# Loads of a graph kernel asked for in small parts, two small jobs moved off GpSimd

## The reference, cut to what matters

```python
N_NODES = 3125; N_EDGES = 103125; EMB = 128; EDGE_F = 16     # dst sorted; every node has its own edge too
def _gin_conv(x, src, dst, edge_attr, w1, b1, bn_w, bn_b, w2, b2, ew, eb):
    edge_emb = edge_attr @ ew.T + eb
    agg_x = segment_sum(x[src], dst, n) + x
    agg_e = segment_sum(edge_emb, dst, n) + eb
    h = concatenate([agg_x, agg_e], axis=1) @ w1.T + b1
    h = (h - mean) * rsqrt(var + BN_EPS) * bn_w + bn_b       # over the nodes
    return relu(h) @ w2.T + b2
h = maximum(layernorm(x), 0)
for l in range(5): h = _gin_conv(h, ...); if l < 4: h = relu(h)
return x + h
```

## Time and profile before

| | |
|---|---|
| median of 3 runs | 663.9 us (662.63 to 664.17) |
| profiled execution, its own time | 669.72 us |
| its span | 667.9 us |
| PE busy, share of the span | 90% |
| DVE, ACT, POOL busy | 50%, 39%, 11% |
| granted TensorE clock, mean | 0.968 |

### The profile page before, as it was taken

The page is one execution under the profiler, slowest core; times in us unless marked ns, Lnnn a source line. Parts: engine busy times, 40 slices in busy tenths (PEclk is TensorE's granted clock), DMA queues, the critical chain, the costliest instruction groups (busy, mean ns, idle before and its releaser), DMA issues.

```text
span 667.9 us, 12631 instructions
## 1 busy us (share of the span) xinstructions
PE 602.1 (90%) x5319; PEld 370.4 (55%) x5319; DVE 331.5 (50%) x663; ACT 260.9 (39%) x569; POOL 71.9 (11%) x90
## 2 busy tenths in 40 slices
PE   4788798969999887999997999997999998999976
PEld 3666687745555544844446644456544458444456
DVE  6897999989999817422113421124411225101034
ACT  0277967746676716502115411127211227012142
POOL 5450136500222100000000000000000000000000
PEclk9798999998999988999998999998999998999999
DMA  6980000000000000100000100000100000100033
GB/s 189 315 227 6 2 4 27 6 5 3 5 4 3 4 6 1 28 5 1 1 2 1 32 1 1 2 1 1 32 1 1 1 2 1 32 1 1 1 98 96
DMA packets 13320, 19.22 MB, mean 29 GB/s; under 512 B 2263, under 2 KB 7397, under 8 KB 13251
## 3 DMA queue, kind: packets, MB, share of 16 engines
q1 hardware_dynamic: 12099, 16.00, 7.9%
q0 software_dynamic: 1152, 2.20, 1.5%
HBM read 16.26 MB, written 1.60 MB: 27 GB/s over the span
## 4 chain that ended last, share of the span: by engine, by line
PE 59%; DVE 2%; ACT 1%; issue 0%; POOLq 0%; DVEq 0%
PE bank L1309 39%; PE bank L1373 10%; PE bank L1345 8%; PE bank L1339 2%; ACT h L1426 1%; DVE bn_stats L1530 1%; DVE h L1551 0%; DVE h L1552 0%; PE bank L1356 0%; PE bank L251 0%; DVE h L1571 0%; ACT bn_small L1439 0%; DVE bn_small L1545 0%; DVE bn_small L1544 0%; DVE bn_small L1546 0%
## 5 line engine op out<-in xcount | busy, mean ns | idle before, releaser
L1309 PE MATMUL bank<-adj,h_pieces 128*128 128x504 bf16 (+1 forms) x1372 | 263.5, 351 | 0.0
L1309 PEld LDWEIGHTS bank<-adj,h_pieces 128*128 128x128 f16 x1372 | 123.0, 97 | 141.4 <-issue 10.2
L1530 DVE BATCH_NORM_STATS2 bn_stats<-bank 128x6 f32<-128x504 f32 (+1 forms) x70 | 42.8, 627 | 220.3 <-PE bank L1345 219.7
L965 ACT ACTIVATE adj<-bank 128x450 bf16<-128x450 f32 x175 | 95.4, 548 | 67.5 <-PE bank L828 54.3
L1417 ACT ACTIVATE aggT<-bank 128x504 f32<-128x504 f32 x24 | 14.2, 590 | 261.0 <-PE bank L1345 223.7
L852 PE MATMUL bank<-h,adj 128*17 128x40 f32 (+11 forms) x1752 | 78.8, 205 | 16.8 <-DVE h L638 11.7
L443 DVE TENSOR_TENSOR h<-iota_lo,h 128x1536 bf16<-128x1536 bf16 (+2 forms) x95 | 87.5, 921 | 8.3 <-PE bank L828 7.2
L828 PE MATMUL bank<-h 128*128 128x75 bf16 x1064 | 69.2, 201 | 19.7 <-DVE h L443 17.3
L452 PE MATMUL bank<-adj,h_pieces 128*128 128x450 bf16 x343 | 83.4, 355 | 1.6 <-issue 1.6
L828 PEld LDWEIGHTS bank<-h 128*128 128x128 bf16 x1064 | 55.0, 99 | 51.0 <-DVE h L443 30.4
L1373 PE MATMUL bank<-weights,h 128*128 128x128 f32 (+1 forms) x500 | 66.7, 302 | 18.3 <-DVE h L1552 18.3
(11 more groups left out here) (145 smaller groups left out, 332.0 us busy)
## 6 DMA issues: line engine op xcount, KB each, us to landing
adj<-attr SPq DMA_DIRECT2D x1, 2524.5 KB
adj<-attr SPq DMA_DIRECT2D x1, 1963.5 KB, 15.3
weights<-wpack SPq DMA_DIRECT2D x5, 323.0 KB
out<-h SPq DMA_DIRECT2D x6, 256.0 KB
adj<-attr SPq DMA_DIRECT2D x1, 1402.5 KB, 7.4
adj<-attr SPq DMA_DIRECT2D x2, 561.0 KB, 5.1
h<-mpack SPq DMA_DIRECT2D x5, 179.0 KB
adj<-order SPq DMA_DIRECT2D x2, 202.0 KB, 3.3
```

Of the source, the lines that this page charges most:

```text
L965: nc.scalar.activation(out_view(u), bank_view(n % CNT_BANKS), ACT.Copy).then_inc(s_ev, 1)
L1309: last = nc.tensor.matmul(agg_ps[b][:, 0:w], hp[:, k, s, :], adj[:, k, c * LW:c * LW + w], start=(k == 0 and s == 0), stop=stop and s == p ...
L1530: V.bn_stats(stats[:, h, ds(c * 6, 6)], w1_ps[b][h][:, 0:cols]).then_inc(st_last if last and h == 1 else st_done, 1)
```

## The change

1. Attributes: 13 parts of two tiles. Parts 0 and 1 as before, part 2 where the old part 2 was; each later part, of tiles from k, is asked for by SyncE when TensorE has done attribute step 3k-12.
2. x: the host lays it out by partition and pads it, so that a load is contiguous in each partition. Four parts (6, 6, 6 and 7 tiles), asked for after steps 6, 8, 10 and 12; ScalarE waits part by part. The memset of the last tile goes. At the end x_res is one transfer.
3. The stores of the starts and the loads of the ranges are issued after step 24, the picked columns after step 38; the weights after all that.
4. GpSimd asks for `rows(b)` when strip 2(b-2) is counted, for `pairs(b)` when strip 2(b-2)+5 is. `block_starts(b)` moves from strip b+6 to 2(b-2)+5, `keys(b)` from 2b+14 to 2(b-2)+12, for b from 2 to 8.
5. Own edges: `add_own` and its waits go. TensorE adds them in PSUM: one or two matmuls at the end of each strip's counts (197 in all, 77 of them in strips 0 to 68), the identity as weights, 18 columns of a padded identity as moving operand.
6. `low_piece` 0 to 5 goes to VectorE, at strips 42, 46, ... 62.
7. `edge_weights_f` of the later layers shares memory with `bound_parts`.

```diff
-ATTR_PARTS = ((0, 2), (2, 4), (4, 9), (9, 16), (16, 25))
+ATTR_PARTS = [(k, min(k + 2, NODE_TILES)) for k in range(0, NODE_TILES, 2)]
+X_PARTS = ((0, 6), (6, 12), (12, 18), (18, 25))
+ATTR_AHEAD, X_EVERY, STARTS_AFTER = 12, 2, 24
+def rows_strip(b):
+    return 2 * (b - 2)
 def starts_strip(b):
-    return b + 6 if b >= 2 else -1
+    return rows_strip(b) + 5 if b >= 2 else -1
+def pairs_strip(b):
+    return rows_strip(b) + 5
 def keys_strip(b):
-    return 2 * b + 14 if b >= 2 else 3
+    return rows_strip(b) + 12 if b >= 2 else 3
...
                     sp.wait_ge(s_pair[0], 16)
-                    attr_rows(2)
-                    sp.wait_ge(s_zero, 1)
-                    sp.dma_start(x_st[:, 0:NODE_TILES - 1, :], ...
-                    sp.dma_start(x_st[0:LAST_ROWS, NODE_TILES - 1, :], ...
-                    for m in range(3, len(ATTR_PARTS)):
-                        attr_rows(m)
+                    parts = 2
+                    for i in range(STEPS):
+                        if parts < len(ATTR_PARTS) and i == max(3 * ATTR_PARTS[parts][0] - ATTR_AHEAD, 0):
+                            if i > 0:
+                                sp.wait_ge(s_step, i)
+                            attr_rows(parts)
+                            parts += 1
+                        for j in range(len(X_PARTS)):
+                            if i == LEAD + X_EVERY * j:
+                                sp.wait_ge(s_step, i)
+                                x_rows(j)
+                        if i == STARTS_AFTER:
+                            store_starts()
+                        if i == PICK_AT + LEAD:
+                            spread_picks()
...
-                    for b in range(2, BLOCKS):
-                        rows(b)
-                    for b in range(2, BLOCKS):
-                        pairs(b)
-                    n = 0
                     for u in range(STRIPS):
+                        for b in range(2, BLOCKS):
+                            if u == rows_strip(b):
+                                pool.wait_ge(s_cnt, strip_at(u) + 1)
+                                rows(b)
+                            if u == pairs_strip(b):
+                                pool.wait_ge(s_cnt, strip_at(u) + 1)
+                                pairs(b)
...
-                        if u >= NORM_AT + 4 and (u - NORM_AT) % 4 == 0 and (u - NORM_AT) // 4 < UNITS:
-                            low_piece((u - NORM_AT) // 4 - 1)
-                        while n < len(PIECES_OWN) - 1 and PIECES_OWN[n][2] <= (u + 1) * SC:
-                            add_own(n)
-                            n += 1
... VectorE
+                        i = (u - NORM_AT - 6) // 4
+                        if (u - NORM_AT - 6) % 4 == 0 and 0 <= i < UNITS - 1:
+                            dve.wait_ge(s_hi, i + 1)
+                            V.tensor_tensor(units(hp, i)[:, :, 1, :], units(x_st, i), units(hp, i)[:, :, 0, :],
+                                            ALU.subtract).then_inc(hp_done, 1)
... TensorE, at the end of counts(), own = u
+                        if own is not None:
+                            to = cnt_ps[n % CNT_BANKS][:, 0:SG * AW].rearrange("p (g k m) -> p g k m", g=SG, m=GW)
+                            for k in range(own * SC // P, min((own * SC + SC - 1) // P, NODE_TILES - 1) + 1):
+                                at = SC + own * SC - k * P
+                                last = nc.tensor.matmul(to[:, :, k, :], ident, ident_pad[:, at:at + SC], start=False, stop=True,
+                                                        skip_group_check=True)
                         last.then_inc(s_cnt, 1)
```

More of the change, by code:

```diff
@@ L178, in ln_tiles @@
     return range(2 * (u - at), min(2 * (u - at) + 2, NODE_TILES)) if at <= u else ()
[L181 to L190, removed]
 def agg0_steps(u):
@@ L222, in gin_program @@
         mp = h1[:, 0, COLS - MP_COLS:COLS]
-        ident = sb(whole, "ident", [P, P], BF16)
+        ident_pad = sb(whole, "ident", [P, 2 * SC + P], BF16)
+        ident = ident_pad[:, SC:SC + P]
         m6 = sb(whole, "edge_weights", [SK, HID], BF16)
@@ L400, in gin_program @@
             s_attr = [sem(f"attr_rows{m}_loaded") for m in range(len(ATTR_PARTS))]
-            s_x = sem("x_loaded")
-            s_zero = sem("x_pad_zeroed")
+            s_x = [sem(f"x{j}_loaded") for j in range(len(X_PARTS))]
             s_diag_m = sem("piece_matrices_made")
@@ new lines, in store_starts @@
+                    def store_starts():
+                        sp.wait_ge(s_start, BLOCKS)
+                        sp.dma_start(starts[0:BLOCK0].rearrange("(p b) -> p b", b=1), start_i[0:BLOCK0, 0:1]).then_inc(s_sdram, 16)
+                        for b in range(1, BLOCKS):
+                            sp.dma_start(starts[base_of(b):base_of(b) + GB].rearrange("(p b) -> p b", b=1),
+                                         start_i[0:GB, b:b + 1]).then_inc(s_sdram, 16)
+                        sp.wait_ge(s_sdram, 16 * BLOCKS)
+                        sp.wait_ge(s_step, 3 * SPARE_ROWS)
+                        for at, out in ((0, first_e), (1, next_e)):
+                            sp.dma_start(out, starts[at:at + GROUPS].rearrange("(c j) -> c j", c=CHUNKS)).then_inc(s_ranges, 16)
@@ L495, in _ @@
+                    assert parts == len(ATTR_PARTS)
                     sp.dma_start(wp[:, :], wpack[0]).then_inc(l_wp, 16)
                     sp.dma_start(mp, mpack[0]).then_inc(l_mp, 16)
[L499 to L511, removed]
@@ L534, in _ @@
                                    allow_small_or_imprecise_dtypes=True).then_inc(s_thr, 1)
-                    nc.gpsimd.memset(x_st[:, NODE_TILES - 1, :], 0.0).then_inc(s_zero, 1)
-                    nc.gpsimd.memset(ident[:, :], 0.0).then_inc(s_ident0, 1)
+                    nc.gpsimd.memset(ident_pad[:, :], 0.0).then_inc(s_ident0, 1)
                     nc.gpsimd.memset(ones[:, :], 1.0)
@@ L818, in transposes, with counts @@
                         last.then_inc(s_tr, 1)
-                    def counts(n, batch, first, tiles):
+                    def counts(n, batch, first, tiles, own=None):
                         pe.wait_ge(s_oh, batch + 1)
@@ L872, in _ @@
                             transposes(BLOCKS)
-                        counts(strip_at(u), batch_at(u), u % PAIR * SG, SG)
+                        counts(strip_at(u), batch_at(u), u % PAIR * SG, SG, u)
                         if u + LEAD < STEPS:
@@ L989, in _ @@
                         for k in ln_tiles(u, SUMS_AT):
-                            if k == 0:
-                                act.wait_ge(s_x, 32)
+                            for j, (a, _) in enumerate(X_PARTS):
+                                if k == a:
+                                    act.wait_ge(s_x[j], 16)
                             nc.scalar.activation(x_st[:, k, :], x_st[:, k, :], ACT.Copy, accum_out=ln_sum[:, k:k + 1]
@@ L1626 @@
     first = np.ascontiguousarray(dst_lin[WIN::WIN].reshape(1, FIRSTS))
+    nodes = np.zeros((NODE_TILES * P, D), np.float32)
+    nodes[:N_NODES] = np.asarray(x)
+    nodes = np.ascontiguousarray(nodes.reshape(NODE_TILES, P, D).transpose(1, 0, 2)).reshape(P, NODE_TILES * D)
     w1, w2 = np.asarray(L0_gnn_W1), np.asarray(L0_gnn_W2)
@@ L1653 @@
     arrays = {
-        "x": np.ascontiguousarray(x), "first": first, "dst_lin": dst_lin, "pair": pair, "order": order,
+        "x": nodes, "first": first, "dst_lin": dst_lin, "pair": pair, "order": order,
         "dst_win": dst_win,
```

45 lines of the change are left out of this document (13 added, 32 removed).

## The result

The changed kernel took 669.8 us in the median of five runs (666.7 to 671.6), the kernel before 662.9 in as many beside it; the ratio of the two is 1.0076, with an interval from 1.0058 to 1.0094. So the change makes the kernel slower, by 5.0 us as the ratio has it (the two medians lie 6.9 us apart; what follows goes by the ratios). The prediction was 660.8 us, faster.

A forecast was written before the change was run, and what follows sets the result against it. VectorE was taken to bound the first stage from 18 to 138 us, TensorE from 158 to 232. Terms -4.7 +0.7 -2.2 +0.8 +3.3 -0.4 -0.6 gave -3.1, so 663.9 became 660.8 us, with 8 in 10 between 656.5 and 667.

The forecast's parts named there:

- The sum: All terms of the change added up: -3.1 us, taken from 663.9 to give 660.8 us.
- The base: Terms counted against the profiled execution (669.72 us), 5.8 us above the runs' median; same difference taken off 663.9.
- Small parts, -4.7: First stage: loads in small parts remove stalls at 27, 29 and partly 51-54 us, and half clock; bounds 0 and -6.
- the stalls stay: Rival: single-word stores delay instructions, so only the 27 and 29 us stalls go; +2.6 on the sum, 663.4; chance 0.20.
- The part after 244 us: Five layers of matmuls at the end of the chain, claimed untouched by the change; no effect booked.
- Rows loads, +0.7: First stage: indirect rows loads issued strip by strip sometimes land late for VectorE; +0.7 us, bounds 0 and +8.
- Low pieces, -2.2: 95 to 138 us: VectorE regains 5.8 us lost to GpSimd's arithmetic, pays 3.6 for six low pieces; bounds -3 and +1.
- Own matmuls, +4.1: First stage: 197 small TensorE matmuls at 30 ns, partly hidden; +3.3 us in the second part, +0.8 in the first.
- The rival of 53 ns: Own matmuls cost 53 ns each, none hidden: 10.4 us, +6.3 on the sum, 667.1; chance of dearer matmuls 0.15.
- the 81 ns of the Trainium skill: Page's price per weight load and matmul pair: own matmuls 11.0 us, estimate 667.7; 0.03 of the dearer-matmuls chance.
- The end, -0.6: End of the first stage: own edge and overflow chain before the last product shortens by 0.33 and 0.24 us.
- the own edges' +0.8 for the first part: Strips 0 to 68: 77 own matmuls at 30 ns, 2.3 us, a third showing on TensorE; range 0 to 2.8.

The follow-up runs named there:

- after_fill34_no_starts_store: Changed kernel with 34 filler matmuls ahead of strip 76 and without stores of the starts and loads of the ranges; 663.2 us, 0.9983.
- before_again: The kernel before, unchanged, run and profiled a second time; 663.4 us, ratio 0.9993, profiled execution 664.16 us.
- loads_only: Kernel before with only the loads in small parts, indirect loads spread, x by partition, and the shared memory; 669.4 us, ratio 1.0093.
- after_fill34: Changed kernel with 34 filler matmuls on TensorE ahead of strip 76, where it waits for VectorE; 665.8 us, ratio 1.0026.
- low_only: Kernel before with only the six low pieces moved from GpSimd to VectorE; 662.3 us, ratio 0.9981.
- own_only: Kernel before with only the own edges moved from GpSimd to 197 small TensorE matmuls, and the shared memory; 669.9 us, ratio 1.0102.
- own_low_fill34: Kernel before with own edges on TensorE, low pieces on VectorE, and 34 filler matmuls ahead of strip 76, loads unchanged; 663.2 us, ratio 0.9971.
- after: The changed kernel with the whole change, against the kernel before; 669.8 us, ratio 1.0076, profiled execution 669.92 us.
- loads_pad: Kernel before with the loads alone in small parts, plus 198 semaphore increments on TensorE (100 before its first matmul, 98 before strip 76); 684.7 us, ratio 1.0311.
- after_pad68: Changed kernel with 68 semaphore increments on TensorE ahead of strip 76; 669.6 us, ratio 1.0084.
- before: The kernel before, without the change, in its first profile; median 662.9 us beside the changed kernel, profiled execution 669.72 us.

## Why the prediction was wrong, step by step

The sum was -3.1 us. Without the two effects that it did not have, the change comes out at -1.1 us against the kernel before (after_fill34_no_starts_store), of which 0.7 is what the missing stores give that kernel too; with them it is +5.0.

**The base.** "It is 5.8 us above the median of the runs, and I take the same difference off 663.9" was the first step that failed. The profile showed 3 us of stall behind the stores, two of 1 us, and a half clock; the runs' median was 5.8 lower. Those two facts belonged together: an execution that is that much above the median has something in it that the median has not. I subtracted the difference and then also booked the removal of the stalls as a gain of 4.7 us. before_again has none of these stalls, so there was nothing of them to gain; 3.6 us of its advantage lie in the first stage.

**Small parts, -4.7.** In the traces, against before_again, loads_only is 0.7 us ahead at the 9th group, 1.2 behind at the 25th and 1.5 behind at the last. The stall behind the stores, of which I took two thirds to go, went the other way: in the new order the stores cost 2.9 us in the runs, in the old 0.7. The rival "the stalls stay" had named the stores of single words, and not the volume, as the cause, and leaving them out bears that out; its price was too low, since it compared with an execution that had the stall already.

**The part after 244 us.** "Five layers of matmuls that the change does not touch" was the largest single term that was missing, 3.3 us by after_fill34, put at nothing without a look at how the layers' code is reached. The instructions of the layers are the same, but they stand elsewhere in TensorE's stream. None of the rivals had this.

**Rows loads, +0.7.** Two waits of VectorE, 2.2 us in all; one of 1.0 stood in the earlier trace rows already, the new one is 1.20 us at 38.73; median landing 3.6 us in place of the 7.7 of the earlier trace rows, nearer to the 2.9 of the earlier trace rows. Near in size.

**Low pieces, -2.2.** L625 takes 610 ns between 95 and 138 us against 782 in the earlier trace rows, and the six pieces 680 each, as forecast. That the low pieces were what slowed it, the single parts show: the same line takes 622 ns in low_only, and still 808 in own_only and 765 in loads_only. low_only's last group starts 2.9 us earlier than before_again's; its runs show 1.3 (0.3 to 2.2). Right in mechanism, and in size within what the two measures leave.

**Own matmuls, +4.1.** Too dear. From the 73rd to the 177th group own_only takes 90.76 us and before_again 89.63: 1.1 us for the 120 or so that I priced at 30 ns, 9 ns each. That is near the bound from below that I had given (11 ns: 18 columns and 3 ns); the weight load of the identity, on which the 30 ns rested, adds nothing that can be seen. The 9 ns is a net figure: GpSimd's additions go at the same time. The timeline says the same: from an own matmul to the product behind it 0.02 us (173.16 to 173.18). The rival of 53 ns, and the 81 ns of the Trainium skill (TensorE: Matmul & The Clock Gate, back-to-back issue gap), given there for 128 columns, find no support in this stream of 18 columns. The runs of own_only (+6.8) do not say this by themselves, since more than the jump may be in them; own_low_fill34, with the same own matmuls and the fillers, is at -1.9. In the first part nothing of their cost shows: own_only is 2.7 us ahead at the 73rd group, which I put down, by argument alone, to GpSimd's additions that no longer slow VectorE.

**The end, -0.6.** own_only takes 13.34 us from its 177th group to the jump's gap (239.28), before_again 13.92 (241.38): -0.6, as forecast.

Of the seven terms of the sum the first was wrong in sign, and the own edges' +0.8 for the first part nowhere shows. The forecast missed because one profiled execution was taken for the usual one, and because a jump was taken for free. The +4.1 for the own matmuls, too dear by about 3 us, erred the other way and made the miss look smaller than it was.

What stays open is how the stores hold up the engines. They do slow the code packets: in all twelve profiled executions that have the stores, one to three packets of q8 took 2.3 to 3.5 us while these were under way, and in the three without them none took more than 1.47. But that a late packet is the stall is not shown. In the changed kernel the packet of 61.98 us took 3.1 us, until 65.10; TensorE had stopped at 61.33, before it left, and worked again at 63.81, before it was there. In the first profile of before no packet of q8 was on its way in the stall from 51 to 54 us (one ended at 50.39, the next left at 57.65). Nor is the stall in every execution of the new order: in the five that were profiled with the stores it stands in three (after, after_fill34, loads_pad; VectorE busy for 2.7 to 3.2 of 5 us) and not in two (loads_only, after_pad68), against one of seven in the old order (before). So the 2.9 us is a mean over executions with and without it, and why the new order has it more often is open.

## What to carry to other kernels

Before a stall of a profile is booked as a gain, compare the profiled execution's time with the median of the runs; if it is higher by about what the stalls add up to, profile once more. Read the profiles of the experiments the same way: several here were over 2 us faster than their medians and do not hold all of the loss. Any edit that adds or removes instructions of TensorE moves the code behind it, and the jump over a skipped branch of an If is where that showed here: look for an "issue" gap in the chain there, and if one appears, shift the code with cheap instructions of the engine in an idle spot ahead of the jump, having measured what they cost. When the parts of a change don't add up to the whole, look for one event that several of them set off.

## What the runs showed of the hardware that I had not expected

- Eight instructions that are never executed cost 4.8 us (1.0073), 128 of them 4.0 (1.0061): a gap of 2.4 or 3.8 us at the jump, and behind it matmuls at the lower clock.
- TensorE's code comes in packets of 16384 bytes, one for about 256 instructions. One takes 0.9 to 1.5 us; while the stores of 4-byte words were under way one to three took 2.3 to 3.5, in every profiled execution that has these stores.
- A semaphore increment on TensorE takes 0.13 us (68 in 9.01 us, all of TensorE's idle time there counted in); 34 pairs of a 128x128 weight load and a one-column matmul take 0.99 us, 29 ns a pair.
- An own matmul of 18 columns with 128x128 weights, between others, adds 9 ns net (1.1 us over 120 of them, own_only against before_again).
- The same kernel's executions differ in where TensorE has the lower clock: 0.66 or 0.83 as the mean over the first 10 us of the second layer (before, before_again), worth 0.9 us.
